# A two-layer transformer kernel: unread bf16 products on TensorE in the attention of layer 0

## The chip, the cores and the metric

The kernel runs on one core of a Trainium2 chip. The metric is the device time of one execution in microseconds (us), lower is better. The engines are named as in the profile: PE (TensorE, the matrix engine; PEld is its weight load), DVE (VectorE), ACT (ScalarE), POOL (GpSimd), SP (the engine whose queue issues nearly all DMAs here). A matmul is told as rows*columns of the stationary operand and rows x columns of the moving one.

## The reference

Input is one sequence of 1024 tokens, width 256. Two transformer layers, each with an attention and a feed-forward part that read the same normalized input:

```python
xn = layernorm(x)
x = x + attn0(xn) + ffn0(xn)      # 16 heads of 16, rope, causal softmax; ffn0: sign weights, relu, hidden 1024
xn = layernorm(x)
x = x + attn1(xn) + moe(xn)       # 16 heads (64 + 64 for scores, 128 for values), gated scores; 32 experts, top 4
```

The change touches the attention of layer 0 alone: scores = (q k^T) / 4 with rope, causal mask, softmax over the keys, times v.

## The kernel before

The kernel is a sequence of blocks; each block gives every engine its own instruction list, and the next block starts when all engines have ended the one before.

`project_layer0` (first block): layer norm, transposes, the products for q, k and v, rope, and the feed-forward of layer 0. PE's last work are the "down" products (L453): for each of 8 token tiles 32 products with 256 columns. DVE scales each result (L380) and adds it to x (L383). q and k go through memory and come back in pairs of heads into `q_buf` and `k_buf` (which are the tiles `spare`, `xT_hi`, `xT_lo`).

`attend_layer0` (second block) works on 8 pairs of heads, p = 0 to 7. For each pair:

- "max": 12 units (`MAX_UNITS`) of scores with queries on the partitions (L680, 48 rows of the array for each head, the two heads in the two halves of the array), with the mask added by small bf16 products (L662, 64 rows). DVE reduces each unit to row maxima (L621, 128x2 from up to 128x1024). There are two slots in PSUM, so PE can be two units ahead of DVE.
- "shift": the maxima are combined (DVE L625), transposed by PE (L691), split by ACT (L594) and DVE (L630), and SP stores them with four small DMAs (L566) as one further row of q. The exponentials of the pair wait for these DMAs.
- "exp": 9 steps of two products each (one for each head) with keys on the partitions (L708, 50 rows), masked likewise (L659), then two exponentials on ACT (L603) into `probsT`. Three PSUM banks are used in turn.
- "mix": for each group of two pairs (four heads) 4 pieces for query half c=0 and 8 for c=1: the products of `probsT` with `v_all` (L726, 128 rows, four heads side by side in the columns), all into bank 7 (`O_BANK`). When a half is complete, DVE takes it out (L638 "take", L641 "invert", L644 "divide", L650 "average"), ACT rounds it (L609) and POOL keeps the remainder (L584).

The order of the steps on each engine is written out by sorting steps by a place in "pair time": max n of pair p stands at p - 1.4 + n/13, shift at p - 0.4, exp n at p + n/9, so the maxima of a pair are worked out while the exponentials of the pair before it run. The pieces of mix for the first group start at 1.2 and spread over 1.62 pair times:

```python
LEAD = 1.4
MIX_FROM, MIX_SPAN, MIX_GAP = 1.2, 1.62, 0.12
for name, at in ordered(max_steps(0) + shift_steps(-0.2) + exp_steps(0) + pieces):   # PE's order
```

`join_layer0` (third block): ACT rounds the output weight (L774), DVE keeps its remainder (L798), then PE does 96 products with 256 columns (L832) on the heads, DVE adds them to x; then the second layer norm, transposes (L840) and the router (L854). `layer1` is the rest of the run, from about 272 us on.

`halves` is a small constant in SBUF, 128 x 2 x 2 x 128 in bf16: identity and mask cut in halves. `half_ident` and `half_mask` are views of it.

## Time and profile before

| | us |
|---|---|
| median of 3 runs | 996.51 |
| lowest and highest of them | 993.98, 1004.88 |
| the profiled execution | 1002.6 |
| its span from first to last instruction | 1000.8 |
| PE busy in it | 874.6 (87%) |
| DVE busy | 635.3 (63%) |
| ACT busy | 421.8 (42%) |
| POOL busy | 343.8 (34%) |
| mean granted clock of PE | 0.919 |

In rows of the timeline the columns are start, duration (both us), engine, line, operation with output and inputs, count, and in brackets the idle time before it with what ended it; a row with a count over 1 is several instructions merged.

### The profile page before, as it was taken

What the parts mean: (1) busy time and instruction counts of PE and PEld (TensorE: products, weight loads), DVE (VectorE), ACT (ScalarE), POOL (GpSimd) and SP (SyncE); (2) the same over time, 40 slices, a digit from 0 to 9 for tenths busy, and PEclk for the clock granted to TensorE, in tenths of its full rate; (3) what the DMA queues carried; (4) which work ended last, traced back from release to release, by engine and by line L of the source; (5) the groups of instructions that cost most, each with busy time, mean ns of one, the idle gap of its engine ahead of it and who ended that gap; (6) DMA issues with size and microseconds to landing.
All of it is one profiled execution on the core that took longest, in us unless ns stands there. A gap on an engine that the chain in (4) does not pass through costs nothing.

```text
span 1000.8 us, 17106 instructions
## 1 busy us (share of the span) xinstructions
PE 874.6 (87%) x5280; PEld 605.1 (60%) x5280; DVE 635.3 (63%) x1179; ACT 421.8 (42%) x959; POOL 343.8 (34%) x333
## 2 busy tenths in 40 slices
PE   3697998886777777899999999999999999999665
PEld 2584544434555665576676676676767667667444
DVE  5697658753578546557656756756666666676552
ACT  3230546674322133435534625635535544543230
POOL 2340000001043675624423424324323433435780
PEclk9896559997878788999999999999999999999778
DMA  6550222420030111404413323422432331341221
GB/s 246 197 153 27 70 71 81 120 71 23 22 117 11 63 66 40 132 22 156 131 52 121 131 79 126 130 80 89 131 115 89 128 118 52 122 150 37 59 77 55
DMA packets 52773, 94.08 MB, mean 94 GB/s; under 512 B 6980, under 2 KB 27980, under 8 KB 52460
## 3 DMA queue, kind: packets, MB, share of 16 engines
q1 hardware_dynamic: 49660, 85.16, 26.7%
q0 software_dynamic: 3072, 8.39, 2.6%
q8 instruction: 24, 0.39, 0.2%
q14 instruction: 17, 0.14, 0.0%
HBM read 75.43 MB, written 24.78 MB: 100 GB/s over the span
## 4 chain that ended last, share of the span: by engine, by line
PE 48%; DVE 3%; issue 2%; POOL 2%; ACT 1%; POOLq 0%; DVEq 0%; ACTq 0%
PE bank L1841 10%; PE bank L1761 9%; PE bank L1711 7%; PE bank L1824 5%; PE bank L1751 4%; PE bank L1865 4%; PE bank L1733 3%; PE bank L1877 2%; PE bank L1858 1%; POOL d_gathered L1648 1%; DVE d_swap L1388 1%; PE bank L1764 1%; PE bank L1874 1%; DVE d_rot L1388 1%; PE bank L1749 0%
## 5 line engine op out<-in xcount | busy, mean ns | idle before, releaser
L1627 POOL TENSOR_SCALAR d_probs<-d_probs,d_row_inv 128x1024 f32<-128x1024 f32 (+7 forms) x128 | 99.3, 780 | 191.7 <-DVE d_row_inv L1416 190.8
L1268 ACT ACTIVATE d_probs<-bank,d_neg_max 128x1024 f32<-128x1024 f32 (+7 forms) x128 | 95.9, 753 | 104.4 <-DVE d_neg_max L1411 104.1
L1841 PE MATMUL bank<-d_pT,d_v 128*128 128x512 f32 (+3 forms) x384 | 130.9, 491 | 0.4 <-ACT d_pT L1315 0.4
L1411 DVE TENSOR_REDUCE d_neg_max<-bank 128x1 f32<-128x1024 f32 (+7 forms) x128 | 95.7, 753 | 51.4 <-PE bank L1764 50.7
L1315 ACT COPY d_pT<-bank 128x512 f32<-128x512 f32 x192 | 86.2, 488 | 80.2 <-PE bank L1824 80.2
L1841 PEld LDWEIGHTS bank<-d_pT,d_v 128*128 128x128 f32 x384 | 72.8, 192 | 59.6 <-issue 47.3
L621 DVE TENSOR_REDUCE b_maxes<-bank 128x2 f32<-128x1024 f32 (+2 forms) x96 | 89.0, 949 | 29.7 <-PE bank L662 20.1
L1824 PE MATMUL bank<-ident,d_probs 128*128 128x128 f32 x576 | 88.5, 285 | 15.3 <-POOL d_probs L1627 10.4
L1761 PE MATMUL bank<-d_k_hi,d_q_hi 128*128 128x512 f32 x192 | 78.3, 408 | 18.8 <-POOL d_k_lo L1621 14.2
L603 ACT ACTIVATE b_probsT<-bank 128x512 f32<-128x512 f32 x132 | 72.2, 594 | 48.3 <-PE bank L659 37.3
L1621 POOL TENSOR_TENSOR d_q_lo<-d_rot,d_q_hi 128x512 fp32r<-128x512 f32 x32 | 40.9, 1279 | 138.1 <-ACT d_q_hi L1264 138.1
L1824 PEld LDWEIGHTS bank<-ident,d_probs 128*128 128x128 f32 x576 | 66.8, 145 | 34.2 <-POOL d_probs L1627 12.9
L1761 PE MATMUL bank<-d_k_hi,d_q_lo 128*128 128x512 f32 x192 | 68.6, 358 | 0.0
L1761 PE MATMUL bank<-d_k_lo,d_q_hi 128*128 128x512 f32 x192 | 68.3, 356 | 0.0
L584 POOL TENSOR_TENSOR heads_lo<-acc,heads_hi 128x512 fp32r<-128x512 f32 x8 | 10.2, 1276 | 160.1 <-ACT heads_hi L609 160.1
L1711 PE MATMUL bank<-xT_hi,d_qkw_hi 128*128 128x512 f32 x128 | 57.5, 449 | 8.4 <-DVE d_slot_hT L1581 4.5
L1761 PEld LDWEIGHTS bank<-d_k_hi,d_q_hi 128*128 128x128 f32 x192 | 38.1, 199 | 38.1 <-issue 17.7
L1401 DVE TENSOR_TENSOR d_rot<-d_rot,d_swap 64x512 f32<-64x512 f32 x64 | 55.7, 871 | 6.7
L1564 DVE TENSOR_TENSOR d_head_lo<-bank,d_head_hi 128x512 fp32r<-128x512 f32 x32 | 22.1, 692 | 59.5 <-ACT d_head_hi L1323 59.3
L1388 DVE TENSOR_TENSOR d_swap<-bank,d_sin 32x512 f32<-32x512 f32 x64 | 44.4, 693 | 19.1 <-PE bank L1711 17.8
L1386 DVE SCALAR_TENSOR_TENSOR d_swap<-bank,d_gs_now,d_sin 32x512 f32<-32x512 f32 x64 | 48.2, 753 | 11.2 <-PE bank L1711 9.3
L1711 PE MATMUL bank<-xT_hi,d_qkw_lo 128*128 128x512 f32 x128 | 51.6, 404 | 0.0
(276 smaller groups left out, 2019.2 us busy)
## 6 DMA issues: line engine op xcount, KB each, us to landing
d_expert_w<-in_expert_w SPq DMA_DIRECT2D x102, 320.0 KB, 3.2
d_slot_x<-slot_x SPq DMA_DIRECT2D x51, 128.0 KB, 2.9
slot_y<-d_slot_y SPq DMA_DIRECT2D x49, 128.0 KB, 3.3
qk_raw<-in_w_qk SPq DMA_DIRECT2D x16, 256.0 KB, 3.3
slot_x<-in_zeros SPq DMA_DIRECT2D x5, 768.0 KB, 5.9
slot_x<-in_zeros SPq DMA_DIRECT2D x3, 896.0 KB, 6.4
d_vw_raw<-in_w_v SPq DMA_DIRECT2D x9, 256.0 KB, 3.2
q_stack<-a_part_hi SPq DMA_DIRECT2D x4, 512.0 KB, 5.1
```

The source lines that it names most:

```text
L603: nc.scalar.activation(probs(head, n), bank[:, E_BANK + t % 3, :], ACT.Exp, scale=SCALE0).then_inc(exped, 1)
L621: nc.vector.tensor_reduce(maxes[:, p % 2, c, :, i], bank[:, first:first + 2, 0:w], AX_X, ALU.max, negate=True).then_inc(maxed, 1)
L1268: nc.scalar.activation(probs[s % NP_][:, 0:width(s)], score_bank(s, width(s)), ACT.Exp, bias=neg_max[:, h.col(s)], accum_out=row_sum[:, h. ...
L1315: nc.scalar.copy(pT[c][:, j:j + blocks, col:col + P], bank[:, T_BANK + tu % 2, 0:blocks * P].rearrange("p (b q) -> p b q", b=blocks)).then ...
L1388: return nc.vector.tensor_tensor(dst, src[rows, :], table[rows, cols], ALU.mult)
L1401: nc.vector.tensor_tensor(rot[n % 2][DS:P, :], rot[n % 2][DS:P, :], swap[DS:P, :], ALU.add).then_inc(rotated, 1)
L1411: nc.vector.tensor_reduce(neg_max[:, h.col(s)], score_bank(s, width(s)), AX_X, ALU.max, negate=True).then_inc(maxed, 1)
L1627: nc.gpsimd.tensor_scalar(probs[s % NP_][:, 0:width(s)], probs[s % NP_][:, 0:width(s)], row_inv[:, h.col(s)], 1.0, ALU.mult, ALU.mult).the ...
L1711: last = nc.tensor.matmul(out, parts(a, k), b[:, k, cols], start=(k == 0 and n == 0), stop=(k == KT - 1 and n == 2))
L1761: last = nc.tensor.matmul(out, a["q"][:, rows], b["k"][:, cols], start=(n == 0), stop=(n == 2 and not diagonal))
L1824: last = nc.tensor.transpose(bank[:, T_BANK + tu % 2, b * P:(b + 1) * P], probs[n % NP_][:, (j + b) * P:(j + b + 1) * P], ident[:])
L1841: last = nc.tensor.matmul(bank_of(h, "pv", n)[:, q:CH], v[:, j, h.hh, :], pT[c][:, j, q:CH], start=(j == 0), stop=(j == len(pieces) - 1))
```

## The change

It adds products that nobody reads, in four places:

- 14 behind the down products of `project_layer0`, into bank 0, without a wait in front of them;
- one behind each of the 12 max units of pair 0 (`KEEP_UNITS`; at -1.4 + (n + 0.5)/13), into bank 7;
- 31 at -0.38 + 0.05 n of pair time (`KEEP_STEP`), that is from -0.38 to 1.12, into bank 7;
- 20 (`AFTER`) at the end of `attend_layer0`, behind a wait for the last take out of bank 7.

Each has a stationary operand of 128*128 (`halves[:, 0, 0, :]`) and a moving one of 128x512 (all of `halves`), both bf16. No product of the kernel is taken away or moved against the others, and no other engine gets or loses an instruction. The views `half_ident` and `half_mask` are now made inside `attend_layer0`.

```diff
--- before.py
+++ after.py
@@ -144,7 +144,7 @@
             heads_hi = sb("heads_hi", [P, NG, T], F32R, on=layer0)
             heads_lo = sb("heads_lo", [P, NG, T], F32R, on=layer0)
             with ExitStack() as b:
-                attend_layer0(nc, b, sb, bank, ident, halves[:, 0, :, :], halves[:, 1, :, :], v_all, rope_scratch,
+                attend_layer0(nc, b, sb, bank, ident, halves, v_all, rope_scratch,
                               heads_hi, heads_lo, q_buf, k_buf,
                               acc[:].rearrange("p k (c t) -> p (k c) t", c=NC), early["pair_in"], d["zeros"], moe)
             with ExitStack() as c:
@@ -454,9 +454,12 @@
                                                 down_sign[:, u, :], start=(u == 0 and q == 0),
                                                 stop=(u == UT - 1 and q == 1))
                 last.then_inc(down_done, 1)
-
-
-def attend_layer0(nc, ctx, sb, bank, ident, half_ident, half_mask, v_all, rope_scratch, heads_hi, heads_lo, q_buf, k_buf,
+            for n in range(14):
+                nc.tensor.matmul(bank[:, 0, :], halves[:, 0, 0, :], halves[:].rearrange("p a f c -> p (a f c)"),
+                                 start=True, stop=True)
+
+
+def attend_layer0(nc, ctx, sb, bank, ident, halves, v_all, rope_scratch, heads_hi, heads_lo, q_buf, k_buf,
                   room, pair_in, zeros, moe):
 
 
@@ -509,7 +512,9 @@
     taken, inverted, divided, averaged = sem("taken"), sem("inverted"), sem("divided"), sem("averaged")
     heads_hi_done, heads_lo_done = sem("heads_hi_done"), sem("heads_lo_done")
 
+    half_ident, half_mask = halves[:, 0, :, :], halves[:, 1, :, :]
     LEAD = 1.4
+    KEEP_UNITS, KEEP_STEP, AFTER = 12, 0.05, 20
 
     def ordered(found):
         return [(name, n) for _, name, n in sorted(found, key=lambda step: step[0])]
@@ -524,6 +529,12 @@
         return [(p + (n + lag) / NE_, "exp", (p, n)) for p in range(NPR) for n in range(NE_)]
 
     MIX_FROM, MIX_SPAN, MIX_GAP = 1.2, 1.62, 0.12
+
+    def keep_steps():
+
+        first = [-LEAD + (n + 0.5) / RING for n in range(KEEP_UNITS)]
+        later = [1 - LEAD + 0.02 + KEEP_STEP * n for n in range(int((MIX_FROM + LEAD - 1 - 0.04) / KEEP_STEP))]
+        return [(at, "keep", 0) for at in first + later]
 
     def mix_places():
 
@@ -664,8 +675,16 @@
                     done.then_inc(last, 1)
 
             pieces = [(at, "mix", place) for place, at in MIX_PLACE.items()]
-            for name, at in ordered(max_steps(0) + shift_steps(-0.2) + exp_steps(0) + pieces):
-                if name == "max":
+            def keep_busy(n):
+
+                for _ in range(n):
+                    nc.tensor.matmul(bank[:, O_BANK, :], halves[:, 0, 0, :], halves[:].rearrange("p a f c -> p (a f c)"),
+                                     start=True, stop=True)
+
+            for name, at in ordered(max_steps(0) + shift_steps(-0.2) + exp_steps(0) + pieces + keep_steps()):
+                if name == "keep":
+                    keep_busy(1)
+                elif name == "max":
                     p, n = at
                     q, k = q_buf[p % NB], k_buf[p % NB]
                     i, c = MAX_UNITS[n]
@@ -728,6 +747,8 @@
                                                 stop=(j == len(pv_pieces(c)) - 1))
                     if j == len(pv_pieces(c)) - 1:
                         last.then_inc(mixed, 1)
+            pe.wait_ge(taken, NG * NC)
+            keep_busy(AFTER)
 
 
 def join_layer0(nc, d, ctx, sb, bank, x, ident, heads_hi, heads_lo, xT_hi, xT_lo, acc, moe, early):
```

## Rows read from the trace of the kernel before

**Rows 1.** The page, the span in 40 slices of 25 us: granted clock of PE in tenths.

```profile
PEclk9896559997878788999999999999999999999778
```

**Rows 2.** Windows: stretch, length, busy us (count) of each engine, PEclk, DMA share, GB/s.

```profile
80.00:84.00 4.00, 2.37 (x26) 1.40 (x26) 3.16 (x6) 0.00 (x0) 0.00 (x0) 1.00 0.01 2
84.00:93.00 9.00, 4.95 (x31) 2.58 (x31) 7.98 (x10) 0.00 (x0) 0.00 (x0) 0.52 0.01 2
93.00:98.00 5.00, 4.22 (x29) 2.30 (x29) 3.75 (x6) 1.54 (x2) 0.00 (x0) 0.50 0.02 3
98.00:108.00 10.00, 9.13 (x66) 5.30 (x66) 7.73 (x8) 5.43 (x10) 0.00 (x0) 0.50 0.22 79
118.00:148.00 30.00, 29.88 (x203) 12.18 (x199) 16.30 (x21) 12.15 (x24) 1.27 (x1) 0.50 0.29 88
158.00:168.00 10.00, 8.29 (x95) 4.02 (x97) 9.32 (x13) 6.13 (x13) 1.28 (x1) 1.00 0.57 161
```

**Rows 3.** Timeline of ACT: the shift of pairs 0 to 4, one per pair.

```profile
93.37 0.26 ACT L594 CAST b_shift_hi<-bank 16x128 fp32r<-16x128 f32 x1 [25.63 <-PE bank L691]
...
108.67 0.26 ACT L594 CAST b_shift_hi<-bank 16x128 fp32r<-16x128 f32 x1 [1.44 <-PE bank L691]
...
128.29 0.26 ACT L594 CAST b_shift_hi<-bank 16x128 fp32r<-16x128 f32 x1 [1.57 <-PE bank L691]
...
152.16 0.26 ACT L594 CAST b_shift_hi<-bank 16x128 fp32r<-16x128 f32 x1 [1.10 <-PE bank L691]
...
167.88 0.26 ACT L594 CAST b_shift_hi<-bank 16x128 fp32r<-16x128 f32 x1 [1.06 <-PE bank L691]
```

**Rows 4.** Waits of PE alone between 84 and 93 us: total, times, longest.

```profile
PE bank L680 <- DVE b_maxes L621: 2.9, 4, 0.9
PE bank L691 <- DVE b_maxes L625: 1.6, 1, 1.6
```

**Rows 5.** Timeline where `attend_layer0` begins.

```profile
78.86 0.28 PE L453 MATMUL bank<-a_down_sign,a_part_lo 128*128 128x256 f32 x1
...
79.64 0.48 DVE L383 SCALAR_TENSOR_TENSOR x<-token_x,a_outs,x 128x256 f32<-128x256 f32 x1
...
80.44 0.33 PE L680 MATMUL bank<-spare 48*128 48x128 f32 x2 [1.31 <-PEq L267]
```

**Rows 6.** Timeline of the router products with 512 columns, at the high clock.

```profile
265.81 0.40 PE L854 MATMUL bank<-xT_hi,c_wr_lo 128*34 128x512 f32 x1
266.04 0.39 PE L854 MATMUL bank<-xT_lo,c_wr_hi 128*34 128x512 f32 x1
```

**Rows 7.** Timeline of PE, the first exponential products of pairs 0 and 3.

```profile
98.34 0.77 PE L708 MATMUL bank<-spare 50*128 50x512 f32 x2
...
158.10 0.48 PE L708 MATMUL bank<-spare 50*128 50x512 f32 x2
```

**Rows 8.** Timeline from the last take to the block `join_layer0`.

```profile
235.45 0.72 DVE L638 STREAM_TRANSPOSE acc<-bank 128x512 f32<-128x512 f32 x1 [7.47 <-PE bank L726]
...
236.95 0.71 DVE L650 STREAM_TRANSPOSE acc<-acc 128x512 f32<-128x512 f32 x1
...
238.39 1.26 POOL L584 TENSOR_TENSOR heads_lo<-acc,heads_hi 128x512 fp32r<-128x512 f32 x1 [5.86 <-ACT heads_hi L609]
...
239.98 1.04 ACT L774 CAST c_wo_hi<-wo 128x1024 fp32r<-128x1024 f32 x1 [1.67 <-PEq L557]
```

**Rows 9.** Timeline of the 96 products L832: numbers 1, 26, 27 and 96.

```profile
242.34 0.58 PE L832 MATMUL bank<-c_wo_hi,heads_hi 128*128 128x256 f32 x1 [6.95 <-DVE c_wo_lo L798]
...
247.84 0.41 PE L832 MATMUL bank<-c_wo_hi,heads_lo 128*128 128x256 f32 x1
248.05 0.37 PE L832 MATMUL bank<-c_wo_lo,heads_hi 128*128 128x256 f32 x1
...
256.40 0.28 PE L832 MATMUL bank<-c_wo_lo,heads_hi 128*128 128x256 f32 x1
```

**Rows 10.** Windows around the end of `attend_layer0`, columns as in rows 2.

```profile
236.00:238.00 2.00, 0.00 (x0) 0.00 (x0) 1.56 (x4) 0.30 (x1) 0.00 (x0) 1.00 0.00 0
238.00:242.00 4.00, 0.00 (x0) 0.00 (x0) 0.94 (x1) 1.56 (x3) 1.26 (x1) 0.50 0.18 45
242.00:248.00 6.00, 5.67 (x26) 5.67 (x27) 1.41 (x5) 1.32 (x2) 0.00 (x0) 0.50 0.22 66
```

## The prediction, made before the changed kernel had run

> **What bounds the kernel now.** I read the page first: PE is the busiest engine, and in its slices the granted clock is below full in the slices from 75 to 150 us (0.7, 0.5, 0.5 in the second row of tenths) although PE is not idle there [rows 1]. So the question is what layer 0's attention loses to the low clock and whether unread products can buy it back. The windows by stage show it. From 80 to 84 us PE is busy 2.37 of 4.00 us at 1.00, the next 9 us run at 0.52, so it fell to 1.2 GHz about 84.5 us; before it fell PE had only the scores of pair 0's maxima, 48 rows of the array, in short bursts between waits for DVE [rows 2, 4]. It then stays low for over 60 us, also from 118 to 148, where PE is busy 29.88 of 30 us; later, with the same kinds of steps, it is at 1.00 and stays there [rows 2]. The price is read from the shift of each pair on ACT, a mark that every pair passes once: 93.37, 108.67, 128.29, 152.16, 167.88. The distances are 15.3, 19.6, 23.9 and then 15.7 us [rows 3]. Pairs 2 to 3 and 3 to 4 hold the same steps; one ran at 1.2 GHz and one at 2.4 GHz, and that is 8.2 us. In the slow pairs PE is the bound (29.88 of 30 us). In the fast ones it shares the bound with DVE: from 158 to 168 us PE is busy 8.29 and DVE 9.32 of 10 us [rows 2]. While only the maxima of pair 0 run, DVE is the bound (7.98 of 9 us), and PE waits for it [rows 2, 4].
>
> Nothing of the rest of the kernel runs beside this stretch, so what it gains or loses reaches the end of the span one for one.
>
> **Price of one filler.** No row shows a bf16 product with 512 columns. The nearest are the router's products with 512 columns: from 265.81 to 266.04, 0.23 us apart at the high clock [rows 6]. At the low clock I take twice that less what doesn't scale, from the products with 256 columns: 25 distances in 5.50 us, 0.22 each [rows 9], so 0.43 us for 512 columns. Their weight loads lie beside the product before, as PEld's do in the windows (4.02 against 8.29 us). Upward the price is bounded by twice the 0.121 us of a warm product with 256 columns, 0.24 [rows 9]; downward I allow 0.20, an estimate, since the weights don't change from one filler to the next. I use 0.23. (The Trainium skill, "TensorE: Matmul & The Clock Gate", section "Back-to-back issue gap", gives N/2.4 + 2.5 ns, 216 ns for N=512; by it the 14 products below would be 3.0 instead of 3.2 us.)
>
> **Part 1, 14 products behind the down products.** The last down product starts at 78.86, and the next block's first one at 80.44, because DVE works until 79.64 + 0.48 = 80.12 and the block change takes 0.32 more [rows 5]. With 14 x 0.23 = 3.2 us behind 78.98, and some 0.2 us of pipeline, PE ends at 82.4 and the block starts at 82.7. Only 1.3 us were cover, so this costs 2.3 us on the path (1.9 with 0.20 us each, 2.4 with 0.24). DVE, ACT and the DMAs of pairs 1 and 2 sit behind the same block change, and none of them is late for another reason.
>
> **Part 2, 12 products between pair 0's maxima.** They fall into PE's idle time: PE is busy 4.95 of 9 us there, with 2.9 and 1.6 us of waits for DVE [rows 2, 4]. Two slots ahead of DVE are enough for 0.23 us: cost 0. If the clock stays up, DVE no longer waits for PE's slow products; DVE's idle time there is 9.00 - 7.98 = 1.0 us, of which I count 0.6 as gain (0 to 0.9).
>
> **Part 3, 31 products at pair times -0.38 to 1.12.** The 8 before pair time 0 run while pair 0's exponentials wait for the DMAs of the shift (ACT 93.37 to PE 98.34, 5.0 us [rows 3, 7]), and PE has only six units of maxima there: cost 0, and no gain either. The other 23 come to 5.3 us of PE time at the high clock, and stand where no mix piece is. By stretch:
> - First exponential of pair 0 to the shift of pair 1, now 98.34 to 108.67, 10.3 us. The like stretch at the high clock is 158.10 to 167.88, 9.8 us, DVE busy 9.32 of 10 [rows 2, 3, 7]. That one holds a take-to-average chain of DVE, 235.45 to 237.66 in the row of the last, 2.2 us [rows 8], which pair 0 lacks; PE has 12 fillers (2.8 us) instead of three mix pieces of about the same size. Between 9.8 and 7.6 us; I take 8.6, gain 1.7 (0.5 to 2.7).
> - Shift of pair 1 to shift of pair 2, 19.6 us: 11 fillers (2.5 us) until 1.12, then a first part of mix. Not over the 15.7 of a full fast pair with its chain unless the fillers weigh more than mix does; not under some 13, DVE's 12.0 busy us with its usual gaps. I take 15.0, gain 4.6 (3.5 to 6.5).
> - Shift of pair 2 to shift of pair 3, 23.9 us: no fillers any more, the same steps as the pair behind it: 15.7, gain 8.2. The condition is that the clock holds without fillers, as it does from 152 us on.
>
> **Part 4, the wait and 20 products at the end.** The wait for the last take ends at 235.45 + 0.72 = 236.17; nothing is queued behind it on PE but the fillers. 20 x 0.23 = 4.6 us and the pipeline end PE at 241.0, where POOL ended the block at 238.39 + 1.26 = 239.65 [rows 8]. POOL's, DVE's and ACT's work covers 3.5 us, and the next block starts 1.3 us late (0.7 to 1.5). What it can buy: the first 26 of the 96 products of the join ran at 1.2 GHz, 242.34 to 248.05, 5.7 us; the other 70 are 0.121 apart, so 26 would be 3.1 us, gain 2.6 [rows 9, 10]. But PE is still idle from 241.0 to 243.7, while ACT and DVE split the weight (239.98 to 242.34, 2.4 us). Before, PE was idle from 235.4 and the clock was still up in 236:238 and down in 238:242 [rows 10]: it fell after an idle time of much the same length. I count half of it, 1.3 us, so part 4 comes to 0 (1.9 us less to 1.5 more).
>
> **Sum.** 0.6 + 1.7 + 4.6 + 8.2 - 2.3 - 0 = 12.8 us less. The profiled execution took 1002.6 us (span 1000.8), so it would take 989.8. It stands 6.1 us above the median of the three runs, 996.51, which span 11 us among themselves; 996.5 - 12.8 gives **984 us** for the median. With the bounds of the terms the gain is 6 to 18 us, so 978 to 990. If a usual run has a shorter low stretch than the profiled one, the gain is smaller, since only what runs at the low clock can be won; that is a reason for the upper half of this range.
>
> **Rivals.**
> - *The fillers make PE the bound.* The clock holds, but the 5.3 us of the 23 late fillers land wholly on the path, because each stands in PE's order ahead of a product that ACT or DVE waits for. For it: PE is busy 8.29 of 10 us in a fast stretch. Against it: busy includes pipeline ends, DVE has 9.32 of these 10. It would leave 15.1 - 5.3 - 2.3 = 7.5 us of gain: 989.
> - *The clock falls all the same, but comes back earlier.* It falls in the gap at pair 0's shift (1.6 us of waiting for DVE) or in the wait for the DMAs, and the full-array fillers bring it back before 128 us, as 26 products on all 128 rows did from 242 to 248 [rows 9, 10]. Then the first two stretches gain nothing, and the 20 or so fillers run at 0.43: 8.2 + 2 - 2.3 - 1, about 7 us: 990.
> - *Slower: the clock stays low whatever PE does until some 150 us.* For it: 30 us of a full PE didn't lift it [rows 2]. Then the 23 fillers cost 23 x 0.43 = 9.9 us on a PE that is the bound, part 1 its 2.3 and part 4 a net 0: 12 us more, 1009. It decides if the clock is not back by about 118 us, where mix begins: from there the rest of pair 1 to 2 and the 8.2 us of the next pair can just pay for these 12. Against it: the steps there use 48 or 50 rows and 32 columns of the array for each product; the fillers use all of it, and products on all rows did lift it elsewhere.
> - *The change doesn't do what it says:* the low stretch is a fault of the record, PE ran fast anyway, and fillers only cost: 2.3 + 5.3 x 0.5, about 1001. The durations speak against it: the first exponential product takes 0.77 us at 98.34 and 0.48 at 158.10 [rows 7], so the clock is real.
>
> The Trainium skill speaks against the change twice, in the same page. Its section "What's actually happening" has the clock go up once PE has been busy, and down once it has been idle, and by that rule the full PE after 98 us would lift it without any filler, and the fillers would only cost. The rows disagree, 29.88 of 30 us busy at 0.50, so it gets no chance of its own. Its section "Seeing it yourself" warns that the records of the clock can be wrong and that it has been seen stuck low for over 50 us; the first is my last rival, the second my slower one.
>
> **How the numbers follow.** A difference under 1%, 10 us, is about what a measurement of this kernel can't tell from none. Chances: forecast 0.60 (984, of which 0.5 below the 1% bound of 986.5), fillers on the path 0.10 (989), fall and early return 0.13 (990), slower 0.12 (1009), record at fault or a loss elsewhere, such as another pattern of the clock in layer 1, 0.05 (1001). Faster by over 1%: 0.5 from the forecast and 0.08 from the scatter of the next two, 0.58. Slower: most of its case, 0.10. Within 1%: 0.32. Range 975 to 999: it takes in the forecast with its bounds and both cases at 989 and 990, a little of scatter, and leaves out the slower case.
>
> **What the profile would show.** PEclk at 1.00 in every window from 79 to 235 us. The first scores of the second block near 82.7. 12 and 31 bf16 products 128x512 with ends 0.23 apart, and DVE's maxima of pair 0 no longer apart than 0.3 us. Shifts on ACT near 95.1, 108.7, 123.7, 139.4 and 155.1. PE's last filler near 240.8 - 12.8 = 228, POOL's end before it, and the first of the 96 products under 2.4 us after the block change, 0.12 or 0.21 apart. The prediction is wrong if a window between 84 and 128 shows 0.50, or if the two stretches of pairs 0 and 1 are over 10 and 16 us at a clock of 1.00, which would be fillers on the path, or if layer 1 (from the first expert work to the end) changes by more than 3 us.

## The result: 1.9% slower, and the profile after

The changed kernel takes 1016.56 us in the median of four runs (1014.85 to 1020.88) against 996.38 us for four of the kernel before (993.98 to 1004.88): the ratio is 1.019, 95% interval 1.014 to 1.024. Its profiled execution took 1018.2 us, with a span of 1016.4 us against 1000.8. The forecast was 984. In all that follows, ratios compare fast executions, those at most 1.5% above the fastest of their kernel (one of 1485.53 us is among those left out), while medians are of all of them, and the two profiles with drawn weights and with 30 late fillers are of executions beyond that bound.

The page's row of granted clock shows first that the clock was not held. Each digit is a 40th of the span, 25.4 us, so the fourth to sixth stand for 76 to 152 us: 8, 5, 5, where [rows 1] has 6, 5, 5 (the prediction read its first as 7).

```profile
PEclk9898559997987789899999999999999999999879
```

The shifts of the pairs on ACT, the marks of [rows 3], pairs 0 to 3 and pair 7:

```profile
99.00 0.26 ACT L605 CAST b_shift_hi<-bank 16x128 fp32r<-16x128 f32 x1 [28.67 <-PE bank L710]
...
122.94 0.26 ACT L605 CAST b_shift_hi<-bank 16x128 fp32r<-16x128 f32 x1 [1.97 <-PE bank L710]
...
149.13 0.26 ACT L605 CAST b_shift_hi<-bank 16x128 fp32r<-16x128 f32 x1 [1.57 <-PE bank L710]
...
166.91 0.26 ACT L605 CAST b_shift_hi<-bank 16x128 fp32r<-16x128 f32 x1 [1.06 <-PE bank L710]
...
229.98 0.26 ACT L605 CAST b_shift_hi<-bank 16x128 fp32r<-16x128 f32 x1 [1.07 <-PE bank L710]
```

Pair 0 to 1 takes 23.9 us instead of 15.3, pair 1 to 2 26.2 instead of 19.6, pair 2 to 3 17.8 instead of 23.9. The windows of the changed kernel, columns as in [rows 2], show where the time goes:

```profile
85.20:92.80 7.60, 6.34 (x49) 3.12 (x50) 6.41 (x8) 0.00 (x0) 0.00 (x0) 0.98 0.01 3
92.80:99.00 6.20, 5.21 (x23) 1.83 (x21) 4.89 (x6) 0.00 (x1) 0.00 (x0) 0.50 0.00 0
99.00:107.00 8.00, 7.67 (x39) 3.01 (x41) 4.81 (x6) 1.53 (x2) 0.00 (x0) 0.50 0.29 100
...
125.00:149.00 24.00, 23.28 (x137) 9.96 (x138) 11.25 (x12) 8.48 (x16) 0.00 (x0) 0.50 0.24 67
...
230.00:236.00 6.00, 3.91 (x50) 1.79 (x50) 1.76 (x5) 4.46 (x9) 0.00 (x0) 0.99 0.14 45
236.00:248.00 12.00, 11.11 (x76) 3.82 (x72) 2.73 (x5) 5.93 (x11) 1.27 (x1) 0.50 0.16 57
262.00:270.00 8.00, 5.87 (x49) 5.87 (x50) 3.93 (x8) 2.35 (x3) 0.00 (x0) 1.00 0.21 70
```

The clock stays up 7.3 us from the first scores (85.22 to 92.5), where it stayed 4 us in the first profile of the kernel before (80.44 to 84.4), and falls beside a PE that is busy 6.34 of 7.60 us. From there the fillers run at 1.2 GHz on an engine that is full (23.28 of 24 us from 125 to 149), and DVE and ACT wait for it. A second fall comes at 236 us in the last pair. The first output products of the join, from 264 us on, are at 1.00 where they were at 0.50.

The two block changes. First the last down product, the 14 fillers (the row merges 13 of them; the record of one, the first by its weight load, is missing), and the first scores:

```profile
81.61 0.28 PE L453 MATMUL bank<-a_down_sign,a_part_lo 128*128 128x256 f32 x1
...
81.96 2.97 PE L458 MATMUL bank<-halves 128*128 128x512 bf16 x13
...
85.22 0.33 PE L699 MATMUL bank<-spare 48*128 48x128 f32 x2 [0.30 <-PEq L267]
```

Down product to first scores is 3.6 us, against 1.6 us in [rows 5]: 2.0 us. The 14 by themselves (duration in ns: least, middle, most; then first and last start):

```profile
L458 PE MATMUL bank<-halves x13: 379/379/379, 82.0 to 84.5; 128*128 128x512 bf16 x13
```

Each lasts 0.38 us, so the 13 starts lie (2.97 - 0.38)/12 = 0.216 us apart. And the end, as in [rows 8] and [rows 9]:

```profile
256.24 0.72 DVE L649 STREAM_TRANSPOSE acc<-bank 128x512 f32<-128x512 f32 x1 [9.28 <-PE bank L745]
...
257.24 4.26 PE L681 MATMUL bank<-halves 128*128 128x512 bf16 x19 [1.07 <-DVE acc L649]
...
261.77 1.04 ACT L795 CAST c_wo_hi<-wo 128x1024 fp32r<-128x1024 f32 x1 [2.68 <-PEq L568]
...
264.13 0.39 PE L853 MATMUL bank<-c_wo_hi,heads_hi 128*128 128x256 f32 x1 [2.63 <-DVE c_wo_lo L819]
264.35 0.28 PE L853 MATMUL bank<-c_wo_hi,heads_lo 128*128 128x256 f32 x1
```

From the last take to the next block 5.5 us against 4.5: 1.0 us. Then all 96 products are at the high clock: the last starts at 275.63, 11.5 us after the first, against 14.1 us: 2.6 us back.

**The account of the 15.6 us between the two profiles:** 2.8 before the change's first instruction (the down products begin at 66.79 instead of 64.03, not the change's doing); 2.0 for the 14; 0.9 more at the shift of pair 0 (13.78 us from the first scores instead of 12.93); 8.6; 6.6; -6.1; 0.0 for pairs 3 to 7; 6.1 between the shift of pair 7 and the last take (26.3 us instead of 20.2, the fall at 236 us); 1.0; -2.6; and -3.7 for all behind the last output product, which is what is left to make 15.6. The clock is up at other moments there too; that this is the reason was not taken apart.

**What a lone filler costs.** Six rows of the changed kernel, three at the high clock and three at the low one, from the mask products over the filler to the next scores:

```profile
86.13 0.26 PE L673 MATMUL bank<-halves 64*128 64x128 bf16 x4
86.33 0.39 PE L681 MATMUL bank<-halves 128*128 128x512 bf16 x1
86.65 0.44 PE L699 MATMUL bank<-spare 48*128 48x384 f32 x2
...
93.94 0.38 PE L673 MATMUL bank<-halves 64*128 64x128 bf16 x4
94.26 0.61 PE L681 MATMUL bank<-halves 128*128 128x512 bf16 x1
94.80 0.79 PE L699 MATMUL bank<-spare 48*128 48x512 f32 x2
```

and the same steps without a filler in the kernel before, which the prediction did not look at:

```profile
94.37 0.39 PE L662 MATMUL bank<-halves 64*128 64x128 bf16 x4
94.56 0.67 PE L680 MATMUL bank<-xT_lo,xT_hi 48*128 48x384 f32 x2
...
169.14 0.26 PE L662 MATMUL bank<-halves 64*128 64x128 bf16 x4
169.24 0.42 PE L680 MATMUL bank<-xT_lo,xT_hi 48*128 48x384 f32 x2
```

At the high clock 0.52 against 0.10 us, so 0.42 for one filler; at the low clock 0.86 against 0.19, so 0.67. The streaming of 512 columns is half of the first (0.21) and under two thirds of the second (0.43); 0.2 us come on top where a filler stands alone between products on 48 to 64 rows. In a row they are 0.216 us apart. The Trainium skill, "TensorE: Matmul & The Clock Gate", section "The mechanism" of its Part 3, says that a weight load overlaps running products only where the row groups differ; by that rule the filler, whose weights take all rows, waits for the products before it and holds up the load of those behind it, which fits the 0.2 us. It doesn't fit the fillers in a row, all on the same rows: the rule would put them further apart by a weight load, 98 ns in this trace, and there each load starts together with the product before it, 82.176 beside 82.175. So the 0.2 us are measured, and their cause is argued.

### The profile page after: what moved, and what is told of

Its sections match the earlier page's. It is cut to its first block, busy times and chain, and to the rows that moved or that the text cites. A ratio compares the mean times of both kernels' runs of the same rounds, so it can differ in the third digit from the quotient of the medians.

```text
span 1016.4 us, 17253 instructions
## 1 busy us (share of the span) xinstructions
PE 898.1 (88%) x5350; PEld 608.1 (60%) x5357; DVE 634.3 (62%) x1179; ACT 421.7 (41%) x959; POOL 343.6 (34%) x333
## 3 DMA queue, kind: packets, MB, share of 16 engines
q1 hardware_dynamic: 49660, 85.16, 26.3%
## 4 chain that ended last, share of the span: by engine, by line
PE 48%; DVE 3%; issue 2%; POOL 1%; ACT 1%; POOLq 0%; DVEq 0%; ACTq 0%
PE bank L1862 10%; PE bank L1782 9%; PE bank L1732 7%; PE bank L1845 5%; PE bank L1772 4%; PE bank L1886 4%; PE bank L1754 3%; PE bank L1898 2%; PE bank L1879 1%; DVE d_swap L1409 1%; PE bank L1785 1%; POOL d_gathered L1669 1%; PE bank L1895 1%; DVE d_rot L1409 1%; ACT d_probs L1289 0%
## 5 line engine op out<-in xcount | busy, mean ns | idle before, releaser
L1845 PE MATMUL bank<-ident,d_probs 128*128 128x128 f32 x576 | 88.5, 285 | 15.7 <-POOL d_probs L1648 8.5
L1782 PE MATMUL bank<-d_k_hi,d_q_hi 128*128 128x512 f32 x192 | 78.0, 406 | 18.3 <-POOL d_k_lo L1642 14.1
L1782 PEld LDWEIGHTS bank<-d_k_hi,d_q_hi 128*128 128x128 f32 x192 | 38.0, 198 | 37.3 <-issue 17.3
L1409 DVE TENSOR_TENSOR d_swap<-bank,d_sin 32x512 f32<-32x512 f32 x64 | 44.4, 693 | 18.6 <-PE bank L1732 17.2
L1732 PE MATMUL bank<-xT_lo,d_qkw_hi 128*128 128x512 f32 x128 | 51.5, 402 | 0.0
```

The lines of the kernel that those rows point to most:

```text
L1409: return nc.vector.tensor_tensor(dst, src[rows, :], table[rows, cols], ALU.mult)
L1732: last = nc.tensor.matmul(out, parts(a, k), b[:, k, cols], start=(k == 0 and n == 0), stop=(k == KT - 1 and n == 2))
L1782: last = nc.tensor.matmul(out, a["q"][:, rows], b["k"][:, cols], start=(n == 0), stop=(n == 2 and not diagonal))
L1845: last = nc.tensor.transpose(bank[:, T_BANK + tu % 2, b * P:(b + 1) * P], probs[n % NP_][:, (j + b) * P:(j + b + 1) * P], ident[:])
```

## The experiments

All ratios are to runs of the kernel before on the same chip. "Distances" are those between shifts on ACT.

### One part at a time

Four kernels, each with one of the four parts of the change and without the other three. The diff to the changed kernel is that of the second, which also lacks the loop of 14 and the last two lines; the third has `later` in place of `first`, the other two an empty list; the first keeps the loop of 14, the fourth the last two lines.

```diff
-        return [(at, "keep", 0) for at in first + later]
+        return [(at, "keep", 0) for at in first]
```

The 14 behind the down products alone (p1):

> Theory A (the 31 late fillers are the loss: each stands alone between products on 48 to 64 rows and costs PE 0.4 us at the high and 0.67 us at the low clock, not 0.23): the 14 cost only the 2.0 us by which the second block starts later, ratio 1.002, and the clock still falls a few us after the first scores. Rival B (the delay moves every later fall of the clock, and the loss is where the clock falls): this part alone shows a good part of the loss, 5 us or more.

Measured: ratio 1.0028 (0.9983 to 1.0074), distances 15.3, 19.6, 23.9 us as in the first profile before; the clock falls 4 us after the first scores. The profile has no loss beyond the late start but 0.9 us in pair 3 to 4 (16.6 us), where the clock dips from 162 to 166 us. The medians are further apart than the ratio, 1006.09 against 997.92 us, so rival B is not refuted: that the late start makes the executions with more time at the low clock the more frequent ones would give just this, and nothing here shows it or rules it out.

The 12 in pair 0 alone (p2):

> Theory A: about 1 us later at the shift of pair 0, since some run at the low clock, at most 2 us slower in all; the clock falls at latest some 8 us after the first scores. If the fillers of this part were what the clock needs, the fall would not come before the shift, and pairs 0 to 2 would be faster than before. Rival B: as with any other delay, 0 to 5 us slower.

Measured: ratio 0.996 (0.9917 to 1.0004). The clock falls 7.3 us after the first scores instead of 4, before the shift, which comes 13.8 us after the first scores. Behind it the distance of pairs 0 to 1 is 15.3 us as before. Its profiled execution was short (span 991.8 us), and the clock rose at 122 us, early in the mixing; the second profile of the kernel before, below, shows how far that moment moves by itself.

The 31 late ones alone (p3):

> Theory A: this part is nearly the whole loss. 23 fillers x 0.67 us = 15.4 us later at the shift of pair 2, given back by up to 6 us where the clock then rises sooner; 8 to 15 us slower. Rival B: the late fillers cost 0.23 to 0.43 us each and are partly hidden, at most 5 us.

Measured: ratio 1.0096 (1.0047 to 1.0145), median 1011.88. Pairs 0, 1 and 2:

```profile
94.18 0.25 ACT L602 CAST b_shift_hi<-bank 16x128 fp32r<-16x128 f32 x1 [25.69 <-PE bank L707]
...
118.13 0.26 ACT L602 CAST b_shift_hi<-bank 16x128 fp32r<-16x128 f32 x1 [1.97 <-PE bank L707]
...
144.31 0.25 ACT L602 CAST b_shift_hi<-bank 16x128 fp32r<-16x128 f32 x1 [1.57 <-PE bank L707]
```

23.95 and 26.18 us: the 8.6 and 6.6 us of the whole change, to 0.1 us. So these are the price of the late fillers at the low clock, and the other parts have no share in it. Part of the 15.2 us comes back, here as there: the clock rises at 155 us, 6 us later than in the first profile before, but the work is further behind by more than that, so pair 2 to 3 has more of its work at the high clock (20.2 us instead of 23.9).

The 20 at the end alone (p4):

> Theory A: the block change 1 us later, the 26 first output products at the high clock, 2.6 us less: 1 to 2 us faster than before, ratio 0.998 to 0.999. Rival: the clock falls in the 2.4 us while ACT and DVE split the weight, and this part is 1 us slower.

Measured: ratio 0.9997 (0.9949 to 1.0046). In its profile the block change comes 5.5 us after the last take, 1 us late, and the 96 output products took 12.8 us, the first 13 or so of them at the low clock: the clock was up during the 20, fell in the gap at 241.1 and was back at 244.5, and 1.3 us were bought instead of 2.6. Cost and gain cancel.

### Do the data matter?

All 77 fillers, with drawn weights in bf16 for operands in place of identity and mask (`dense`, copied once by DVE in the first block; the 14 read it too).

```diff
-                    nc.tensor.matmul(bank[:, O_BANK, :], halves[:, 0, 0, :], halves[:].rearrange("p a f c -> p (a f c)"),
+                    nc.tensor.matmul(bank[:, O_BANK, :], dense[:, 0:P], dense[:],
                                      start=True, stop=True)
```

> All 77 fillers as in the changed kernel, same shapes and type, but their operands are drawn weights in bf16 instead of the identity and the mask. Theory D (the operands are nearly all zeros, so the chip hardly counts the products as work): with real data the clock stays at 1.00 from 79 to 235 us and the kernel is 10 us or more faster than the changed one. Theory A (what counts is how much of the time the array streams; the data do not matter): the clock falls 7 to 8 us after the first scores as before, pairs 0 to 1 and 1 to 2 take 23.9 and 26.2 us, ratio to before near 1.015 to 1.02.

Measured: ratio 1.0169 (1.0091 to 1.0248), distances 23.95, 26.2 and 23.9 us, the clock down from 92 us. The clock rose again at 170.5 us, at 154 in the changed kernel. Up to there the data made no difference; theory D falls.

### Is it the density?

Three fillers in place of one at each place of pair 0, the 14, nothing else:

```diff
-                    keep_busy(1)
+                    keep_busy(3)
```

> The 14 behind the down products, and three fillers in place of one behind each of the 12 max units of pair 0; no others. If density in this stretch is what was missing, the clock stays at 1.00 up to the shift of pair 0, about 12 us from the first scores, and falls only in the stretch behind it; then pair 0 to 1 starts warm and is shorter than 15.3 us, down to some 13. Theory A's price: three in a row cost 0.42 + 2 x 0.23, near 0.9 us per unit, close to DVE's 0.95, so at most 3 us later at the shift of pair 0. If the clock falls all the same at 4 to 8 us, density of such products does not hold it.

Measured: ratio 1.0006 (0.9969 to 1.0044). The clock is held as long as the fillers come and falls 3.5 us behind the last, beside maxima without fillers:

```profile
84.00:98.00 14.00, 13.81 (x86) 5.26 (x84) 10.86 (x12) 0.00 (x0) 0.00 (x0) 1.00 0.01 2
102.00:108.00 6.00, 5.34 (x44) 3.41 (x42) 4.71 (x6) 2.17 (x4) 0.00 (x0) 0.50 0.40 135
```

The shift of pair 0 comes 15.5 us after the first scores, 2.6 us late, and pair 0 to 1 takes 15.0. Held and then let go, it buys nothing.

Three at all 43 places, the 14, without the 20:

> 14, and three fillers at each of the 43 places (129), without the 20 at the end. If the clock holds with so many: pair distances show the price of the fillers at 2.4 GHz, 0.42 + 2 x 0.23 us per place, pair 0 to 1 about 20 places x 0.87, so near 22 us, hardly better than now. If it falls: 20 places x (0.67 + 2 x 0.43) = 30 us more for pair 0 to 1 alone, and the kernel is 40 us or more slower than before. Either way not faster than before.

Measured: ratio 1.0101 (1.0033 to 1.0169). The clock stays at 1.00 from 80 us until 199 us, in the windows of pairs 0 to 1 and 1 to 2 too:

```profile
100.00:122.00 22.00, 22.00 (x152) 9.47 (x152) 11.81 (x14) 6.96 (x12) 0.00 (x0) 1.00 0.11 37
122.00:144.00 22.00, 21.14 (x188) 9.23 (x186) 11.90 (x16) 10.41 (x21) 0.00 (x0) 1.00 0.25 74
```

Distances 22.6, 20.8, 15.8 us. So the aim of the change can be met, and the price of meeting it this way eats the gain: PE is busy 22.00 of 22 us at the high clock. The 22.6 us are the 22 foretold, though the 20 x 0.87 of the expectation are 17.4 us and its text doesn't say what makes up the rest.

### What is fixed by the work and what isn't

The kernel before, profiled once more:

> The kernel before once more, for the places where its clock changes. If the moment at which it rises in the mixing (148.7 us in the first profile) is fixed by the work, it is the same again, to 1 us. If it varies, it is elsewhere by several us, and the shift of pair 3 with it, while the distances of pairs 0 to 1 and 1 to 2 at the low clock are 15.3 and 19.6 us again.

```profile
96.38 0.26 ACT L594 CAST b_shift_hi<-bank 16x128 fp32r<-16x128 f32 x1 [25.80 <-PE bank L691]
...
111.68 0.26 ACT L594 CAST b_shift_hi<-bank 16x128 fp32r<-16x128 f32 x1 [1.45 <-PE bank L691]
...
131.29 0.26 ACT L594 CAST b_shift_hi<-bank 16x128 fp32r<-16x128 f32 x1 [1.57 <-PE bank L691]
...
149.04 0.26 ACT L594 CAST b_shift_hi<-bank 16x128 fp32r<-16x128 f32 x1 [1.06 <-PE bank L691]
```

15.3 and 19.6 us again, but 17.75 for pair 2 to 3: the clock rose at 136 us instead of 149, 6 us won without any change. And it was down from 218 to 228 us, in the last pair, where the first profile had it up. The kernel with only the 20 at the end, whose work is the same up to there, had it rise at 135 and down from 217 to 224. In the other kernels in which it had fallen by then it rose anywhere from 122 to 155 us, and at 170.5 with drawn weights. So most of the 8.2 us of pair 2 to 3, the largest term of the forecast, was a draw of that one execution; the 6.1 us in the last pair of the changed kernel are likely another, since such falls come and go. The moment of the first fall varies too: without fillers in pair 0 it comes 1.6 to 4.0 us after the first scores (seven profiles), with one at each of the 12 places 6.5 to 7.3 us (three profiles). What repeats is the distance of pairs 0 to 1 at the low clock, 15.3 us in all five profiles without a filler behind the shift of pair 0 in which the clock was low all through it.

### Fewer places, more at each

Three, and then two, at 12 + 15 places, without the 14 and the 20. The diff is that of two:

```diff
-    KEEP_UNITS, KEEP_STEP, AFTER = 12, 0.05, 20
+    KEEP_UNITS, KEEP_STEP, AFTER = 12, 0.1, 20
-                    keep_busy(1)
+                    keep_busy(2)
```

Three:

> No 14 and no 20; three fillers behind each of the 12 max units of pair 0, then three at each of 15 places (step 0.1 instead of 0.05). Theory A (the clock needs dense products; a place of three costs PE 0.88 us at the high clock): if the clock holds, pair 0 to 1 falls from the 22.6 us of 43 places of three to about 14, pair 1 to 2 from 20.8 to about 16, pair 2 to 3 is 15.8, and the shift of pair 0 comes 15.5 us after the first scores instead of 13: in sum 3 to 8 us faster than before, ratio 0.992 to 0.997. Rival: the clock falls between the places and the fillers cost twice as much, 10 us slower.

Measured: ratio 1.0025 (0.9986 to 1.0065), distances 15.9, 15.7, 15.8 us at 1.00 throughout; the shift of pair 0 is at 15.5. The distances came out as told but for 2 us in the first; the ratio did not. The 2.6 us at pair 0 are whole on the path, and the profile has the clock down for 3.4 us each at 185 and 216 us; how the rest is made up stays open.

Two:

> The same with two fillers at each place instead of three. If the clock holds: 0.23 us less at each of 27 places, of which some 1.5 us at the shift of pair 0 and 2 to 3 us later count, ratio 0.988 to 0.995. If two are too few, it falls within 8 us of the first scores, as with one.

Measured: ratio 0.9947 (0.9903 to 0.9991), median 990.89. Two are enough at these places. The same kernel, measured a second time:

> The version with two fillers at 12 + 15 places once more: ratio 0.995 again if its gain is real, and runs in two groups, near 990 where the clock stays up in pairs 3 to 7 and near 1002 where it falls there.

Measured: ratio 0.9946 (0.9927 to 0.9964), six runs from 988.88 to 991.79, median 990.48. Its shifts and windows:

```profile
95.94 0.26 ACT L602 CAST b_shift_hi<-bank 16x128 fp32r<-16x128 f32 x1 [26.01 <-PE bank L707]
...
110.17 0.26 ACT L602 CAST b_shift_hi<-bank 16x128 fp32r<-16x128 f32 x1 [1.06 <-PE bank L707]
...
124.79 0.26 ACT L602 CAST b_shift_hi<-bank 16x128 fp32r<-16x128 f32 x1 [1.06 <-PE bank L707]
...
140.59 0.26 ACT L602 CAST b_shift_hi<-bank 16x128 fp32r<-16x128 f32 x1 [1.06 <-PE bank L707]
```

```profile
84.00:96.00 12.00, 10.87 (x72) 3.98 (x71) 10.69 (x12) 0.06 (x1) 0.00 (x0) 1.00 0.01 1
98.00:108.00 10.00, 9.69 (x88) 4.47 (x86) 8.60 (x9) 4.35 (x8) 0.00 (x0) 1.00 0.25 82
```

First scores to shift 13.3 us, then 14.2, 14.6 and 15.8: from the first scores (82.63) to the shift of pair 3, 58.0 us, against 71.7 in the first profile of the kernel before and 65.75 in the second. That is 13.7 or 7.8 us less, by which profile of the kernel before is taken; the ratio, over many executions, makes it 5 us. The clock was down from 209 to 220 us in this profile too, so an execution near 990 need not have it up in pairs 3 to 7. The group of runs near 1002 did not show this time; in the first set of 12, three were above 1002.

That version with the 20 at the end as well:

> The version with two fillers at 12 + 15 places, and the 20 at the end as well. Theory A: the block change comes 1 us later and the first 26 output products run at the high clock, 2.6 us less: 1 to 2 us faster than the version without them, ratio to before near 0.993. Rival: nothing gained, since the clock falls in the 2.4 us behind them or is low at the last mix piece already.

Measured: ratio 0.9997 (0.9954 to 1.004), median 1002.07; ten of the twelve runs lie in two groups, near 990 and near 1002. The profile is one of the second: the clock fell in the steady part, where the forecast took it to stay up, and stayed low for 30 us with a full PE; pair 6 to 7 took 23.9 us.

```profile
160.00:176.00 16.00, 14.78 (x169) 6.68 (x167) 11.60 (x16) 10.42 (x20) 1.27 (x1) 1.00 0.35 101
180.00:208.00 28.00, 27.88 (x193) 11.96 (x189) 16.91 (x24) 12.20 (x24) 2.55 (x2) 0.50 0.21 69
```

The fall begins 56 us ahead of the 20 (179.8 and 236.0), so they can't have caused it in this execution; why the slower group was the larger one in this set stays open. Of the 20 themselves the profile shows cost and gain cancel again: the last take to the first output product takes 7.9 us instead of 6.9 in the version without them, and the 96 output products 13.0 instead of 13.9, since the clock is up at their start, falls at 244.7 and is back at 248.1.

Only the 12 places of two:

> Only two fillers at each of the 12 places of pair 0. If it is the 15 later places that hold the clock in pairs 0 to 2, it falls within 4 us of the shift of pair 0 and the distances are about 15 and up to 19.6 us, ratio to before 0.997 to 1.003. If pair 0 alone decides, the clock stays up and the distances are 14 us or less, ratio 0.985 to 0.99.

Measured: ratio 1.0001 (0.9965 to 1.0038); the clock fell at 100 us, 3 us behind the shift of pair 0, distances 15.0, 17.3, 15.8; the 17.3 is under 19.6 because the clock was back at 123.7 us. The later places hold it in pairs 0 to 2. What no run tells is whether they need two at each: 31 single ones and 15 times two are nearly as many products in the same stretch, and every kernel with single ones came to it with the clock already down.

Two more fillers ahead of max units 2, 6 and 10 of pairs 3 to 7, written into the unit's own bank before its scores:

> The version with two fillers at 12 + 15 places, and in pairs 3 to 7 two fillers ahead of max units 2, 6 and 10, written into the unit's own bank before its products. If the clock's falls between 175 and 235 us come from the same want of dense products, they are gone, and the spread of 989 to 1002 us of the version without shrinks to its lower end; the price is 3 x 0.65 us a pair on a PE that is not quite the bound, 0 to 8 us in all. If the falls have another cause they stay, and this is slower by the price.

Measured: ratio 1.0061 (1.0039 to 1.0083). The distances of the later pairs rise from 15.8 to 17.1 us (one, with a dip of the clock, to 18.6), so each of the six fillers of a pair costs 0.22 us net; the six runs lie close together (999.44 to 1004.54), but the profile still has the clock down at 144 and at 220 us. At this density it isn't held there, and it costs more than the falls do: 10.9 us between the medians of this version and the one without, taken side by side (1001.38 and 990.48).

### The price of a filler, taken apart

30 late fillers in 10 places of three, nothing else (step 0.15):

> Only the late fillers, 30 of them in 10 places of three instead of 31 single ones. Theory A (a lone filler costs 0.67 us at the low clock because 0.24 us of weight loads can't hide beside the products of 48 and 64 rows): one such loss per place, 21 x 0.24 = 5 us less than with single ones, so the distance from the shift of pair 0 to that of pair 2 is about 45 us instead of 50.1 (34.9 without fillers). Rival (the price is all streaming): 50 us again.

```profile
96.20 0.26 ACT L602 CAST b_shift_hi<-bank 16x128 fp32r<-16x128 f32 x1 [25.65 <-PE bank L707]
...
119.03 0.26 ACT L602 CAST b_shift_hi<-bank 16x128 fp32r<-16x128 f32 x1 [1.95 <-PE bank L707]
...
141.30 0.26 ACT L602 CAST b_shift_hi<-bank 16x128 fp32r<-16x128 f32 x1 [1.06 <-PE bank L707]
```

45.1 us from pair 0 to pair 2 instead of 50.1, as foretold, but the clock was back at 136 us here, and that has a share in it that I can't take out, so this number is in part luck. In pair 0 to 1 alone, all at the low clock, 21 fillers in 7 places take 22.8 us, 20 in 20 places 23.95: 1.1 us and the 0.43 of one filler for 13 places, 0.12 us each. A loss per place exists, half of what theory A had. Ratio 0.998 (0.9937 to 1.0024).

31 single ones of 128 columns:

> Only the 31 late single fillers, with 128 columns instead of 512. Theory A: 0.24 + 0.11 = 0.35 us each at the low clock, 10.8 us of PE time, of which some 5 hide as with the long ones: shift of pair 0 to that of pair 2 about 40 us. Rival (streaming alone): 31 x 0.11 = 3.3 us, all hidden, 35 us as before.

Pair 0 to 1 takes 18.1 us, all at the low clock; the same with 512 columns 23.95 and without fillers 15.3. With 20 fillers in that stretch, a short one costs 0.14 us net and a long one 0.43; the difference, 0.29, is near the 0.32 of 384 columns at 1.2 GHz, and what is left for a short one, 0.14, is more than the 0.11 of its streaming though part of it hides. Pair 0 to 2 is 38.9 us, told 40. Ratio 1.0055 (1.002 to 1.0091). So it is not streaming alone, all hidden, and a fixed part is there.

## Why the prediction was wrong

**The step that failed** is the condition under part 2 and part 3, "if the clock stays up". One filler per max unit puts the fall off from 1.6 to 4.0 us after the first scores to some 7 and no more, and with the clock down the fillers cost 15.2 us where 15.1 were to be gained. The forecast had argued that products on all 128 rows are of the kind that the clock needs, and left open whether one in each 0.9 us is enough. Two at each of the 12 places are: there the clock is up until 99.8 us, 16 us after the first scores, and two at each of the 15 later places carry it on. The likeliest case was built on a quantity, how dense PE has to be, that no row of the kernel before shows; the rows at hand (low at 29.88 of 30 us busy, high at 8.29 of 10) should have warned that busy time can't tell, and that the case of the low clock deserved far more than 0.12.

Behind its condition the sum was sound. With two fillers at 27 places the first scores to the shift of pair 3 take 58.0 us, 13.7 less than in the profile that the forecast started from, where parts 2 and 3 said 15.1. What it lacked was a bound for its largest term: the 8.2 us of pair 2 to 3 enter the range without one, and against the second profile before, the term is 2.0 us (17.75 and 15.7). The bounds that are given add up to 8 to 18 us, not 6 to 18.

**The slower rival had the right cost, for half the right reason.** That the fillers fall on a PE that is the bound at the low clock is what happened. That the clock stays low "whatever PE does" is not so: two or three fillers at each place held it up. Its sum was near: 23 x 0.43 + 2.3, 12 us, told as 1009; measured 15.6 between the profiles and 20 between the medians. Its terms:

| term | told | measured |
|---|---|---|
| 14 fillers, late start of the block | 2.3 | 2.0 in the profiles |
| price of a filler at the low clock | 0.43 | 0.67 alone between other products; 0.43 to 0.60 net |
| pair 0 to 1 | 12 x 0.43 = 5.2, 8 more free | 8.6 for the 20 |
| pair 1 to 2 | 11 x 0.43 = 4.7 | 6.6 |
| 20 at the end | 1.3 | 1.0 |
| the join's first 26 products | 2.6, half counted | 2.6 in the changed kernel, 1.3 with the 20 alone |

The price of 0.23 us for a filler came from products in a row with 512 columns; it is near for the 14 (0.216, so 3.0 us for all) and wrong for a lone one, 0.42 at the high clock. The step under it was "their weight loads lie beside the product before": so they do for the fillers in a row, but around the lone filler at 86.33 the loads are on record only at 86.32 and 86.65, each at the start of its own product. The last mask product, of 64 columns (0.03 us), had started at 86.21, so 0.1 us is lost ahead of the filler, and 0.1 us behind it, where it is 0.32 us to the next product instead of 0.22. The eight before pair time 0 were to be free beside the DMAs of the shift. They weren't: between the shift of pair 0 and its first exponential product there are 8.1 us instead of 5.0 (99.00 to 107.07), because six units of maxima with eight fillers at the low clock fill PE for longer than the DMAs take.

**The rival of fillers on the path at a held clock** is shown by the run with three at each place: 22.6 and 20.8 us, PE busy 22 of 22. With one at each place it couldn't be seen, since the clock wasn't held.

**Pairs 2 to 3 and after.** "The same steps as the pair behind it: 15.7" is right where the clock is up. But the clock's rise in the mixing is not fixed by the work: 149 us in one profile of the kernel before and 136 in the next. The 8.2 us was thus mostly on offer without any change, and "it holds without fillers, as it does from 152 us on" was read from one execution; another execution of it falls at 218, and its variants at 180, 217 or 236 us.

**Part 4** cost 1.0 us where 1.3 was told, and the toss for 2.6 fell three ways: 2.6 in the changed kernel, 1.3 with the 20 alone, 0.9 with them behind the two fillers. That the 1.3 equals the half that was counted is luck.

**Where the median's 20 us come from:** by the ratios 10 us from the late part alone and 3 from the 14, nothing clear of noise from the others, so some 6 of the 19 are left. By the medians it is 14 and 8, which leaves nothing. Which reading is right isn't shown; for the first one the fall in the last pair, 6.1 us in the changed kernel's profile, is a candidate and only that.

**The record is real:** from the start of a lone filler to the next product's it is 0.54 us in the stretch at 0.50 (94.26 to 94.80) and 0.32 in the one at 1.00 (86.33 to 86.65), so the last rival falls as well.

## What to carry to other kernels

A filler has to be dense enough to hold the clock and cheap enough to pay for it, and both are found by trying: one product at each of 43 places put the fall off by some 4 us and cost 8.6 + 6.6 us, three at each held the clock through the stretch and ate the gain, two at 27 places gave 0.5% less time than the kernel before. Price a filler from where it will stand, between products on other rows, and not from a row of equal products; where it has to stand among such products, several at one place lose less than one at each of many (22.8 us for 21 in 7 places, 23.95 for 20 in 20). And take a second profile of the kernel before counting on a stretch at the low clock: here the moment at which it ends moved by 13 us between two executions of one kernel, and lay between 122 and 170 us over all kernels in which the clock fell in this stretch, and with it the gain.

## What the runs showed of the hardware

- The clock was low for 28 us with PE busy 27.88 of 28, and up with PE busy 14.78 of 16 on the same steps of one execution: the busy time doesn't tell the level. By the Trainium skill, "TensorE: Matmul & The Clock Gate", section "What's actually happening", a sustained busy PE has its clock back; that held here for products on all rows in a row (0.121 us apart after 5.7 us of them [rows 9]) and not for the steps of this attention, where PE was busy 29.88 of 30 us at 0.50 [rows 2] and, with a single filler at each place, 23.28 of 24: the clock came back only 24 to 79 us after its fall in or behind pair 0.
- Between an all-rows bf16 product of 512 columns and products on 48 to 64 rows some 0.2 us are lost, at either clock (0.42 and 0.67 us for one, where its streaming is 0.21 and 0.43); among themselves the former are 0.216 us apart at the high clock.
- Operands of identity and mask and operands of drawn weights gave a fall of the clock 7.3 and 6.5 us after the first scores and the same distances of pairs 0 to 1 and 1 to 2, to 0.1 us.
